# Attention and feed-forward sandwich on one core: first tile loaded by half partitions on two queues, last tile's epsilon on VectorE, last store in halves

## The reference, cut to what matters

```python
x = x + _layernorm(attn(_layernorm(x)))      # first norm of tile 0: the opening of the kernel
x = x + _layernorm(ffn(_layernorm(x)))       # last norm of tile 3: its end

def _layernorm(x, axis=-1, eps=1e-05):
    m = jnp.mean(x, axis=axis, keepdims=True)
    v = jnp.var(x, axis=axis, keepdims=True)
    return (x - m) / jnp.sqrt(v + eps)

# ffn: six times
h = gelu(einsum('bsd,hd->bsh', x, w1) + b1)
x = einsum('bsh,dh->bsd', h, w2) + b2 + x    # and a layer norm with gain and bias after the first five
```

## Time and profile before

| | us |
|---|---|
| median of three runs | 632.46 (632.03 to 632.61) |
| the profiled execution: its own time | 632.11 |
| its span in the profile | 630.3 |
| TensorE busy | 620.9 (99% of the span) |
| VectorE busy | 462.5 (73%) |
| ScalarE busy | 407.1 (65%) |
| GpSimd busy | 251.8 (40%) |
| first transpose of real data starts | 6.59 |
| last store is issued | 628.01 |

### The profile page before, as it was taken

The page is one execution under the profiler, slowest core; times in us unless marked ns, Lnnn a source line. Parts: engine busy times, 40 slices in busy tenths (PEclk is TensorE's granted clock), DMA queues, the critical chain, the costliest instruction groups (busy, mean ns, idle before and its releaser), DMA issues.

```text
span 630.3 us, 9041 instructions
## 1 busy us (share of the span) xinstructions
PE 620.9 (99%) x2913; PEld 518.0 (82%) x2913; DVE 462.5 (73%) x809; ACT 407.1 (65%) x680; POOL 251.8 (40%) x234
## 2 busy tenths in 40 slices
PE   8999999999999999999999999999999999999996
PEld 6878888887888888888888888888888888888886
DVE  6999766977676877677777768766776767677465
ACT  5989986967755666566565656755665665556454
POOL 5685413339225362324432253623255322304033
PEclk9999999999999999999999999999999999999999
DMA  8210000020111020011200110200112000003522
GB/s 289 69 36 0 2 2 0 4 71 34 37 39 40 4 70 6 12 31 37 72 5 2 40 39 15 60 6 7 36 37 72 5 4 5 6 11 77 113 72 68
DMA packets 51599, 24.10 MB, mean 38 GB/s; under 512 B 43104, under 2 KB 47584, under 8 KB 51552
## 3 DMA queue, kind: packets, MB, share of 16 engines
q1 hardware_dynamic: 51264, 23.26, 14.2%
q10 hardware_dynamic: 288, 0.26, 0.1%
HBM read 19.51 MB, written 4.00 MB: 37 GB/s over the span
## 4 chain that ended last, share of the span: by engine, by line
PE 88%; DVE 4%; issue 1%; ACT 1%; POOL 1%; DVEq 0%; ACTq 0%
PE BK L516 44%; PE BK L833 38%; PE BK L634 2%; PE BK L843 1%; PE BK L490 1%; DVE ST L391 1%; DVE BK L616 1%; POOL RN L713 0%; DVE XL L727 0%; PE BK L647 0%; DVE QB L619 0%; DVE OL L625 0%; DVE R L721 0%; DVE MV L394 0%; DVE QB L578 0%
## 5 line engine op out<-in xcount | busy, mean ns | idle before, releaser
L819 ACT ACTIVATE HH<-BK,B 128x512 fp32r<-128x512 f32 x192 | 132.1, 688 | 179.6 <-PE BK L516 177.5
L825 DVE TENSOR_TENSOR HL<-BK,HH 128x512 fp32r<-128x512 f32 x192 | 130.7, 683 | 98.2 <-ACT BK L822 97.5
L516 PE MATMUL BK<-XH,WL 128*128 128x512 f32 x416 | 162.6, 391 | 0.0
L516 PE MATMUL BK<-XL,WH 128*128 128x512 f32 x416 | 162.1, 390 | 0.0
L516 PE MATMUL BK<-XH,WH 128*128 128x512 f32 x416 | 162.0, 389 | 0.0
L833 PE MATMUL BK<-HH,WL 128*128 128x512 f32 x368 | 143.5, 390 | 0.6 <-DVE HL L825 0.6
L833 PE MATMUL BK<-HL,WH 128*128 128x512 f32 x368 | 143.2, 389 | 0.0
L833 PE MATMUL BK<-HH,WH 128*128 128x512 f32 x368 | 143.2, 389 | 0.0
L822 ACT ACTIVATE BK<-BK,B 128x512 f32<-128x512 f32 x192 | 125.4, 654 | 0.0
L516 PEld LDWEIGHTS BK<-XH,WH 128*128 128x128 f32 x416 | 78.1, 188 | 16.5
L516 PEld LDWEIGHTS BK<-XH,WL 128*128 128x128 f32 x416 | 78.1, 188 | 16.2 <-DVE XL L503 0.2
(11 more groups left out here) (136 smaller groups left out, 783.7 us busy)
## 6 DMA issues: line engine op xcount, KB each, us to landing
STG<-in_w SPq DMA_DIRECT2D x24, 512.0 KB, 3.7
G<-sums SPq DMA_DIRECT2D x160, 8.0 KB, 1.7
out<-R SPq DMA_DIRECT2D x16, 128.0 KB, 1.9
X<-in_x SPq DMA_DIRECT2D x3, 512.0 KB, 7.7
R<-turns SPq DMA_DIRECT2D x3, 512.0 KB, 4.2
sums<-P SPq DMA_DIRECT2D x40, 8.0 KB, 1.4
R<-in_wv SPq DMA_DIRECT2D x1, 512.0 KB, 5.8
STG<-in_wo SPq DMA_DIRECT2D x1, 512.0 KB, 6.2
```

Source lines behind the costliest of these rows:

```text
L516: r = e.matmul(dst, s, m, start=first and i == 0, stop=last and i == len(todo) - 1)
L819: lambda e, ev=ev, hs=hs, bias=bias: e.activation(HH[:, hs, :], bank_of[ev][:, :], ACT.Gelu, bias=bias),
L825: lambda e, ev=ev, hs=hs: e.tensor_tensor(HL[:, hs, :], bank_of[ev][:, :], HH[:, hs, :].bitcast(f32), ALU.subtract), ("hlo", n, j))
```

## The change

Tile 0's chunks are each loaded as two halves, partitions 0 to 63 from SP's queue and 64 to 127 from ScalarE's; the statistics of a chunk wait for both. The identity's load goes to ScalarE's queue, behind the halves. In `last_tile` the addition of epsilon to the variance is a `tensor_scalar` on VectorE (key K + 0.55) where it was an activation on ScalarE (K + 0.7), and the tile EPS and its memset on GpSimd go. The last chunk's store goes out in two halves of the partitions, on SP's queue and on ScalarE's, and the program's end waits for both. Instructions whose semaphore nobody waits for no longer increment one.

```diff
-        EPS = sb("EPS", [128, 1])
...
         for c in range(4):
-            load(-100 + c, X[:, 0, c, :], x[0][:, c, :], (f"ldx0{c}",),
-                 engine="sync" if c % 2 == 0 else "scalar")
+            for h, queue in enumerate(("sync", "scalar")):
+                rows = slice(64 * h, 64 * h + 64)
+                load(-100 + 0.5 * c, X[rows, 0, c, :], x[0][rows, c, :], (f"ldx0{c}{queue}",), engine=queue)
...
-        load(-95, ID[:, :], ident_in, ("ldid",))
+        load(-97.5, ID[:, :], ident_in, ("ldid",), engine="scalar")
...
-        op("gpsimd", 60, [], lambda e: e.memset(EPS[:, :], EPS_LN), ("eps",))
...
-            x_in = (lambda c: [(f"ldx0{c}",)]) if t == 0 else (lambda c, t=t: [(f"ldx{t}",)])
+            x_in = (lambda c: [(f"ldx0{c}sync",), (f"ldx0{c}scalar",)]) if t == 0 else (lambda c, t=t: [(f"ldx{t}",)])
...
-                op("scalar", K + 0.7, [("z_mv", n, c), ("eps",)],
-                   lambda e, c=c: e.activation(VE[:, t, c:c + 1], MV[:, t, c, 1:2], ACT.Identity, bias=EPS[:, :]),
+                op("vector", K + 0.55, [("z_mv", n, c)],
+                   lambda e, c=c: e.tensor_scalar(VE[:, t, c:c + 1], MV[:, t, c, 1:2], EPS_LN, 1.0, ALU.add, ALU.mult),
                    ("z_vs", c))
...
-                load(K + 3, out[t][:, c, :], R[:, t, c, :], ("stored", t, c), [("fin0", t, c)])
+                if c < 3:
+                    load(K + 3, out[t][:, c, :], R[:, t, c, :], ("stored", t, c), [("fin0", t, c)])
+                    continue
+                for h, (engine, name) in enumerate((("sync", "stored"), ("scalar", "closed"))):
+                    rows = slice(64 * h, 64 * h + 64)
+                    load(K + 3, out[t][rows, c, :], R[rows, t, c, :], (name, t, c), [("fin0", t, c)], engine=engine)
...
-        op("sync", 1e9, [("stored", NT - 1, 3)], lambda e: None)
+        op("sync", 1e9, [("stored", NT - 1, 3), ("closed", NT - 1, 3)], lambda e: None)
...
+        waited = set()
+        for q in order.values():
+            for o in q:
+                waited.update(w[0] for w in map(resolve, o[2]) if w is not None)
...
-                if done is None:
+                if done is None or done[0] not in waited:
                     continue
...
-                if done is not None:
+                if done is not None and done[0] in sems:
                     last.then_inc(sems[done[0]][0], step)
```

More of the change, by code:

```diff
@@ L922, in sandwich, with resolve @@
         slot_of.update(slots)
+        def resolve(w):
+            return prior[w] if w[0] in ("ring", "slot", "claim", "give") else None if w[0] == "after" else w
+        waited = set()
+        for q in order.values():
+            for o in q:
+                waited.update(w[0] for w in map(resolve, o[2]) if w is not None)
         owner = {}
@@ L936, in sandwich @@
                 place[done] = sems[s][1]
-        def resolve(w):
-            return prior[w] if w[0] in ("ring", "slot", "claim", "give") else None if w[0] == "after" else w
         def issue(eng, name):
```

## The result

The changed kernel takes **633.64 us** (median of 13 executions, 633.32 to 634.06) against 632.24 us (13 executions, 632.03 to 632.61) of the kernel before on the same chips: a ratio of 1.0021, 95% interval 1.0012 to 1.0029, 1.4 us slower. The forecast was 632.5, the range ended at 633.1, and "slower by over 0.2%" had a chance of 0.04.

A forecast was written before the change was run, and what follows sets the result against it. TensorE was taken as busy throughout the middle, leaving only the opening and closing chains. Terms -0.18 + 0.25 - 0.05 = +0.02 us on the profiled 632.11, with the runs' median 0.35 higher, gave 632.5 us, range 631.7 to 633.1.

The forecast's parts named there:

- Chunks by halves: Opening: chunk 0 complete 0.25 us earlier, of which 0.18 us reaches TensorE as gain; halves' queue time costed at nothing.
- The later chunks stay ahead of their readers: Opening: each chunk fills VectorE over 0.5 us, while a queue issues one load in about 0.45 us.
- rival 2: Opening: the first chunk's halves land no earlier than the whole did, so the start gives nothing; 632.7 us, chance 0.17.
- The warm-up as the limit: Opening: warm-up matmuls hold TensorE to 6.40, so the first transpose starts near 6.41 instead of 6.59, gaining 0.18 us.
- The weights' cover: Opening: w_k1 and w_k2 land later but still before ScalarE needs them, by 0.2 and 0.1 us; costed at nothing.
- Rival 3: Opening: late w_k1 holds up ScalarE's copy to XH, 0.73 us later; 633.4 us, chance 0.10.
- Covered by 0.1 us: Opening: w_k2 lands at about 8.58, ahead of its read on ScalarE at 8.69.
- Order of the instructions: Plan unchanged up to the last tile; there it becomes aggregate 3, fin0 1, z_vs 3, fin0 2, fin0 3.
- Rival 4: Middle: the plan changes there after all, by a missed clock; 631.2 to 633.7 us, chance 0.06.
- rival 1: Both ends gain: z_vs 3 ahead of fin0 1, power on time, halved store saves its bound; 632.0 us, chance 0.23.
- Epsilon: Last tile: with the addition on VectorE, fin0 of chunk 3 starts 0.25 us later; bounds 0.05 earlier to 0.30 later.
- Last store: Kernel's end: halving the last store gains 0.05 us; bounds 0.25 earlier to 0.2 later.

The follow-up runs named there:

- open_3296: Kernel before with the change's opening, tile 0's chunks cut at partition 32 instead of 64; 632.39 us, ratio 1.0002.
- open_cols: Kernel before with the change's opening, tile 0's chunks halved by columns instead of partitions on the same two queues; 632.53 us, ratio 1.0006.
- open_c0: Kernel before with only chunk 0 halved, by columns, over both queues; other chunks whole, identity on SP's queue; 632.63 us, ratio 1.0006.
- eps_both: Kernel before with epsilon on VectorE and fin0 of chunks 1 and 2 both ordered behind z_vs of chunk 3; 632.03 us, ratio 0.9999.
- eps_only: Kernel before with only the epsilon addition (z_vs) moved to VectorE, without EPS; 632.11 us, ratio 1.0001.
- best: Kernel before with opening cut at partition 32, epsilon on VectorE, fin0 1 and 2 behind z_vs 3, whole last store; 632.17 us, ratio 0.9998.
- store_cols: Kernel before with only the last store halved, by columns, over the two queues; 632.30 us, ratio 1.0003.
- store_3296: Kernel before with only the last store cut at partition 32 over the two queues; 632.29 us, ratio 1.0002.

## Why the prediction was wrong, point by point

**Chunks by halves: the step that failed.** "What the halves cost is queue time", and I priced it from whole loads, "about 0.47 us a load" on SP and 0.45 on ScalarE. A half of 64 partitions costs 0.58 to 0.62 there (once 0.87), and the load behind it 0.59. So the sentence "The later chunks stay ahead of their readers" was false: chunk 3's statistics were 0.78 late and took the second pair with them. Chunk 0's came at 3.54, so rival 2's sign (no earlier than 3.39) is there as well. I bounded the landing of chunk 0 and the landing of the weights from both sides, but for the issue of a shape that no row showed I took the nearest row as the price and gave it no upper end. Rows that would have given one were in the trace of the kernel before. These are the pieces of 32 partitions that it stores and loads in other patterns:

```profile
L277 SPq DMA_DIRECT2D G<-sums x160: 302/432/1327, 118.7 to 564.4; - x160
L277 SPq DMA_DIRECT2D turns<-TB x8: 502/506/511, 567.3 to 590.8; - x8
```

An issue on SP's queue could take 0.51 or even 1.33 us. The term was -0.18 and measured +0.84 in the trace, 1.0 in the times. Where the issues are cheap it depends on the cut: 0.06 to 0.15 at partition 32 (open_3296), 0.4 and 0.5 by columns (open_cols, open_c0; both intervals just include no difference, both traces have 0.7 to 0.8 at the first UH matmul), and nowhere -0.18, because each chunk now depends on two queues: a gain for the first chunk is given back by the second, or more than that by the fourth. The profile showed that too, had I asked when chunk 1 lands and not only chunk 0.

**The warm-up as the limit** was right as a mechanism (eps_both shows the transposes waiting for it), and its end at 6.40 is not fixed: 0.4 us earlier to 0.9 later in other executions.

**The weights' cover.** Rival 3 put the loss at w_k1 in front of the copy. ScalarE did its high parts of w_q1 and w_k1 from 6.01 to 6.92 and wanted the copy at 7.84: no. The side was right and the place wrong; the late load was chunk 3. That rival 3's 633.4 lies near the measured 633.6 is luck. "Covered by 0.1 us" for w_k2 was wrong too: forecast to land at 8.58, it landed near 10.4, and ScalarE waited 0.59 us for it, though not on the chain to UH.

**Order of the instructions**: as worked out, and the middle didn't move: from the first UH matmul to the first statistics of the last tile it is 611.01 us before and 610.98 after. Rival 4 falls, and so does rival 1, since z_vs of chunk 3 didn't run ahead of fin0 1.

**A reading**: the 7.6 us that I put "behind the last one" begin at 622.7, and the last matmul starts at 625.23, so only 5 us lie behind it. No term of the sum uses this.

**Epsilon**: right in sign, 0.06 instead of 0.25. Two things were mis-sized. The inserted z_vs of chunk 2 cost VectorE nothing, since the statistics of chunk 3 come 1.07 to 1.08 behind those of chunk 2 with it and without; what ends their wait is TensorE. And the 0.81 us isn't a fixed length of the power beside a fin0: it holds a wait for that fin0's end. Started 0.09 nearer to it, the power took 0.72. The sentence that ScalarE "is not what the end waits for" was off as well: the earlier trace rows has the last power waiting for ScalarE's z_vs. What eats that gain is the order. On VectorE z_vs of chunk 3 stands behind a fin0, and in eps_only it starts at 626.46, where ScalarE's started at 626.23; right behind the aggregate, as in *best*, it starts at 626.22.

**Last store**: forecast -0.05 with 0.2 as the worst, measured +0.4. The failed sentence is the bound, again from whole loads. From its issue on, ScalarE's half took 2.3 us to land where the whole store took 1.9; 0.2 of these 0.4 are the longer issue.

**The rule on queues.** By the Trainium skill, "DMA: Bandwidth & Descriptors", section "Issuing engines are not separate DMA queues", neither split gains anything. The runs agree: store_cols, store_3296 and open_c0 gain nothing, and 0.14 us for chunk 0 in open_3296 is all that any split won. The remark there that the sequencer's time is usually small beside the DMA doesn't carry this case: here chunk 3 stood behind three issues on ScalarE's queue, which took 0.76 us longer than the cheap ones of open_3296. A second page of the Trainium skill bears on it, which I hadn't weighed: "SBUF — State Buffer", section "Can I just issue two DMAs to hit both halves?", answers no for one transfer at partition 0 and one at partition 64. The runs agree with that as well: with such halves chunk 0's statistics started at 3.54 and 3.70, no earlier than with whole chunks. Neither page of the Trainium skill has a price for issuing 64 partitions, which is what was lost here.

**The chances.** I gave 0.04 to slower by over 0.2% because the ranges of both splits came from rows of whole, 128-partition DMAs. Two unknown issue prices stood in the sum, and both were wrong the same way. The range also stopped at 633.1, short of the 633.4 that I had worked out for rival 3 with a chance of 0.10.

## What to carry to other kernels

A DMA cut in two is two issues of an unknown shape; before counting on less data, profile one execution and read the issue's length for that shape, and for the load behind it. Where work goes on in chunks, ask of a split not when the first chunk lands but when the last one does: it inherits every issue ahead of it on both queues. On a closing chain, put a short instruction that the chain waits for ahead of longer ones that nobody waits for, and let at most one VectorE instruction with two operands in SBUF stand before a GpSimd instruction that reads SBUF: together that was worth 0.18 us in the trace here and cost nothing, too little to show in the times.

## What the runs showed of the hardware

- Among the loads issued in the first 4 us an issue of 64 partitions took 0.51 to 0.63 us (0.87 once in each of the two executions with that opening, for ScalarE's second load in one and its third in the other), and the issue behind it on the same queue 0.57 to 0.62 (0.85 for the 192 columns), where pieces of 16, 32, 48, 80, 96, 112 and 128 partitions took 0.38 to 0.46 when no 64 stood directly ahead. For the last store it was 0.52 to 0.58 against 0.33 for the whole one. Other things lengthen an issue too: 512 KB loads of 128 partitions took up to 1.36 us at 5.9 us, and no run looked into why.
- A VectorE instruction with two operands in SBUF and a GpSimd instruction that reads SBUF hold each other up. The last power ended 0.41 us behind the end of the fin0 that had started before it in all 17 profiled executions, whatever its own start; the subtraction for w_k1 grew from 0.41 to 1.52 us behind a GpSimd subtraction that had started first, and ended 0.28 us behind it (open_cols, open_c0). The Trainium skill, "SBUF — State Buffer", section "Who interferes with whom", names this pair and calls it an exclusive lock in which the order of issue decides who blocks. The subtractions agree. The power agrees in its wait, but its last 0.41 us held nobody up: in eps_both and best a second fin0 ran beside it for its usual 0.48 us.
- The 13 warm-up matmuls took between 4.57 and 5.92 us in the executions above, because the rate of one each 0.43 us gives way to a faster one (one each 0.23 to 0.24 us) at different times or not at all before their end, though the granted clock reads 1.00 over the first 7 us in all of them.
